# A two-layer attention kernel on one core: new orders for all engines' instruction lists

## What is computed

```python
xf = x.reshape(b, c, n)                       # n = 1024
q = einsum('rc,bcn->brn', Wq, xf) + bq        # 16 rows
k = einsum('rc,bcn->brn', Wk, xf) + bk        # 16 rows
v = einsum('oc,bcn->bon', Wv, xf) + bv        # 128 rows
energy = einsum('bri,brj->bij', q, k)         # 1024 x 1024
attn = softmax(energy, axis=2)
out = gamma * einsum('bcj,bij->bci', v, attn) + x
```

## Time and profile before

| | |
|---|---|
| median of 3 runs | 193.89 us (193.38 to 194.21) |
| the profiled execution | 193.06 us, span 191.3 us |
| TensorE busy | 179.1 us (94% of the span) |
| VectorE busy | 145.7 us (76%) |
| ScalarE busy | 155.5 us (81%) |
| GpSimd busy | 156.9 us (82%) |
| granted TensorE clock | 1.00 |

### The profile page before, as it was taken

The page is one execution under the profiler, slowest core; times in us unless marked ns, Lnnn a source line. Parts: engine busy times, 40 slices in busy tenths (PEclk is TensorE's granted clock), DMA queues, the critical chain, the costliest instruction groups (busy, mean ns, idle before and its releaser), DMA issues.

```text
span 191.3 us, 3482 instructions
## 1 busy us (share of the span) xinstructions
PE 179.1 (94%) x1282; PEld 123.1 (64%) x1282; DVE 145.7 (76%) x137; ACT 155.5 (81%) x223; POOL 156.9 (82%) x120
## 2 busy tenths in 40 slices
...
GB/s 155 345 104 0 215 9 42 69 3 3 2 113 0 5 111 3 0 3 3 110 3 0 3 55 58 2 3 107 61 55 7 55 0 58 3 0 55 55 55 55
DMA packets 3890, 9.51 MB, mean 50 GB/s; under 512 B 548, under 2 KB 932, under 8 KB 3876
## 3 DMA queue, kind: packets, MB, share of 16 engines
...
...
## 4 chain that ended last, share of the span: by engine, by line
PE 34%; POOL 31%; ACT 15%; issue 10%; DMA 4%; DVE 4%; SPq 1%; POOLq 0%; DVEq 0%; ACTq 0%
POOL attn_lo L364 14%; PE out_psum L720 10%; POOL attn_hi L359 9%; ACT ring L472 8%; PE out_psum L722 7%; ACT attn L484 4%; DMA qk_swapped<-qk 4%; PE ring L671 3%; PE ring L697 3%; PE out_psum L756 3%; PE ring L642 2%; DVE neg_max L563 2%; PE ring L624 2%; PE ring L657 2%; ACT attn_hi L490 2%
## 5 line engine op out<-in xcount | busy, mean ns | idle before, releaser
L364 POOL TENSOR_TENSOR attn_lo<-attn,attn_hi 128x1024 fp32r<-128x1024 f32 x37 | 90.4, 2455 | 1.8 <-ACT attn_hi L490 1.3
L563 DVE TENSOR_REDUCE neg_max<-ring 128x1 f32<-128x1024 f32 x64 | 75.6, 1219 | 15.7 <-PE ring L673 15.3
L472 ACT ACTIVATE ring<-ring,neg_max 128x1024 f32<-128x1024 f32 x64 | 69.6, 1087 | 9.9 <-DVE neg_max L563 9.3
L484 ACT ACTIVATE attn<-ring 128x1024 f32<-128x1024 f32 x64 | 63.3, 1024 | 9.8 <-DVE attn_lo L558 5.6
L359 POOL TENSOR_SCALAR attn_hi<-attn 128x1024 fp32r<-128x1024 f32 x35 | 39.2, 1134 | 5.5 <-ACT attn L484 5.4
L699 PE MATMUL ring<-qk_swapped,qk 64*128 64x512 f32 x64 | 29.0, 478 | 0.0
L697 PE MATMUL ring<-qk,qk_swapped 64*128 64x512 f32 x64 | 28.5, 468 | 0.3
L671 PE MATMUL ring<-qk_swapped,qk 64*128 64x512 f32 x56 | 25.1, 452 | 3.4 <-ACT attn L484 1.7
L673 PE MATMUL ring<-qk,qk_swapped 64*128 64x512 f32 x56 | 25.7, 461 | 0.0
L558 DVE TENSOR_TENSOR attn_lo<-attn,attn_hi 128x1024 fp32r<-128x1024 f32 x11 | 19.4, 1778 | 5.5 <-POOL attn_hi L359 4.7
L723 PE MATMUL out_psum<-attn_hi,v_hi 64*128 64x512 f32 x72 | 23.0, 399 | 0.0
...
## 6 DMA issues: line engine op xcount, KB each, us to landing
...
qk<-shift_rows SPq DMA_DIRECT2D x7, 8.0 KB
```

The lines of the kernel that those rows point to most:

```text
L364: nc.gpsimd.tensor_tensor(attn_lo[:, k - 1], attn[:, k], attn_hi[:, k - 1].bitcast(fp32), ALU.subtract).then_inc(cut_made["lo", "gpsimd"], 1)
L472: nc.scalar.activation(e[:], e[:], ACT.Exp, bias=neg_max[s][:, i:i + 1], accum_out=row_sum[s][:, i:i + 1]).then_inc(sum_made, 1)
L484: nc.scalar.activation(attn[:, k], ring_tile("ET", s, k)[:].rearrange("p (a n) -> p a n", a=2), ACT.Exp).then_inc(attn_made, 1)
L563: nc.vector.tensor_reduce(neg_max[s][:, i:i + 1], ring_tile("E", s, i)[:], axis=AX.X, op=ALU.max, negate=True).then_inc(max_made, 1)
```

## The change

Only the five lists are changed, and no function. The same stages, tiles and numbers are computed. Counted by kind and engine:

| | hi | lo | v_hi | v_lo |
|---|---|---|---|---|
| ScalarE | 13 to 4 | | 5 to 4 | |
| GpSimd | 35 to 44 | 37 to 32 | 3 to 4 | 5 to 4 |
| VectorE | | 11 to 16 | | 3 to 4 |

The warm entries ask for 16 pairs of matmuls where they asked for 18. All other kinds stay on their engine in the same number, in another order. In stage 0 the first two energies are E.0.2 and E.0.1, where they were E.0.6 and E.0.0, and QX.1 stands before them. Cut to the two ends of each list:

```diff
 PE_ORDER = """
-raw.0.0.0 raw.0.1.1 E.0.6.2 QX.1.0.0 E.0.0.1 QK.1.0.0 E.0.7.2 warm.0.2 E.0.4.0 E.0.2.1 E.0.1.2 warm.0.2 E.0.3.0
-E.0.5.1 VX.0.0.2 warm.0.2 E.1.4.0 V.0.0.2 shift.0.0.1 warm.0.2 E.1.7.1 warm.0.2 QX.2.0.0 E.1.6.2 QK.2.0.0 warm.0.2
-ET.0.2.1 warm.0.4 ET.0.3.2 warm.0.2 E.1.5.1 ET.0.1.0 E.1.0.2 PH.0.2 E.1.2.0 PH.0.3 shift.0.1.1 E.1.3.2 ET.0.0.1
...
-PV.7.1 PV.7.3 PH.7.5 PH.7.4 PV.7.6 PV.7.5 PV.7.4 PV.7.7
+raw.0.0.0 raw.0.1.1 QX.1.0.2 E.0.2.0 QK.1.0.2 E.0.1.1 warm.0.2 E.0.6.2 E.0.7.0 E.0.0.1 warm.0.2 E.0.3.2 E.0.5.0
+E.0.4.1 warm.0.1 VX.0.0.2 E.1.4.0 V.0.0.2 shift.0.0.1 warm.0.2 E.1.5.1 warm.0.2 QX.2.0.0 E.1.0.2 QK.2.0.0 warm.0.1
+ET.0.1.1 warm.0.4 ET.0.0.2 warm.0.2 shift.0.1.1 ET.0.3.0 E.1.3.1 VX.1.0.2 ET.0.2.0 V.1.0.2 PH.0.1 ET.0.7.0 E.1.7.1
...
+PV.5.4 E.7.2.0 E.7.1.1 PV.5.7 ET.6.6.2 PH.5.5 PV.5.6 PV.5.5 VX.7.0.0 ET.6.7.2 E.7.6.1 V.7.0.0 PH.6.6 PH.6.2 PH.6.4
+ET.6.5.2 shift.7.1.0 ET.6.1.1 PV.6.4 PV.6.7 PV.6.0 ET.7.5.0 ET.7.6.1 ET.7.4.2 PV.6.6 PH.6.5 PH.6.1 PV.6.5 ET.7.2.1
+ET.7.1.2 ET.7.7.0 PH.6.3 PV.6.1 PV.6.2 ET.7.0.2 ET.7.3.0 PV.6.3 PV.7.7 PH.7.6 PV.7.0 PH.7.3 PH.7.5 PH.7.4 PH.7.1
+PH.7.2 PV.7.1 PV.7.5 PV.7.3 PV.7.2 PV.7.4 PV.7.6
 """
 ACT_ORDER = """
-sum.0.6 evac.1.0 sum.0.0 sum.0.7 sum.0.4 sum.0.2 sum.0.1 sum.0.3 log.0.0 sum.0.5 sum.1.4 v_hi.0.0 log.0.1 sum.1.7
-sum.1.6 attn.0.2 attn.0.3 attn.0.1 sum.1.5 sum.1.0 sum.1.2 attn.0.0 sum.1.3 sum.1.1 sum.2.4 attn.0.6 log.1.1 sum.2.7
...
-attn.6.4 attn.6.1 attn.6.6 sum.7.5 log.7.1 hi.6.6 hi.6.4 attn.6.3 attn.6.7 attn.7.3 v_hi.7.0 attn.7.2 hi.7.2
-attn.7.0 attn.7.1 attn.7.6 attn.7.7 attn.7.5 attn.7.4 hi.7.5 hi.7.4
+evac.1.0 sum.0.2 sum.0.1 sum.0.6 sum.0.7 sum.0.0 sum.0.3 sum.0.5 log.0.0 sum.0.4 log.0.1 sum.1.4 sum.1.5 sum.1.0
+attn.0.1 attn.0.0 attn.0.3 attn.0.2 sum.1.3 attn.0.7 attn.0.4 sum.1.7 sum.1.1 sum.1.6 sum.1.2 sum.2.4 log.1.1
...
+sum.7.6 log.7.1 attn.6.1 attn.6.5 attn.7.6 attn.7.4 attn.7.5 attn.7.1 attn.7.7 attn.7.0 attn.7.3 attn.7.2 hi.7.3
 """
 DVE_ORDER = """
-max.0.6 max.0.0 max.0.7 max.0.4 max.0.2 max.0.1 max.0.3 max.0.5 max.1.4 rows.0.0 v32.0.0 max.1.7 max.1.6 mask.2.0
...
-max.7.7 v_lo.6.0 finish.5.1 max.7.5 v32.7.0 lo.6.5 rows.7.1 lo.6.6 lo.6.3 lo.6.4 finish.6.0 v_lo.7.0 lo.7.2
-finish.6.1 lo.7.6 lo.7.5 finish.7.0 finish.7.1
+max.0.2 max.0.1 max.0.6 max.0.7 max.0.0 max.0.3 max.0.5 max.0.4 max.1.4 rows.0.0 v32.0.0 max.1.5 max.1.0 mask.2.0
...
+finish.5.0 max.7.3 v32.6.0 max.7.2 max.7.1 v_lo.6.0 finish.5.1 max.7.6 v32.7.0 lo.6.6 rows.7.1 lo.6.2 lo.6.5
+v_lo.7.0 lo.6.1 finish.6.1 finish.6.0 lo.7.5 lo.7.1 lo.7.3 lo.7.4 finish.7.0 finish.7.1
 """
 POOL_ORDER = """
-mask.1.0 stack.1.0 parts.0.0 parts.0.1 v_lo.0.0 hi.0.2 hi.0.3 hi.0.1 lo.0.2 lo.0.3 lo.0.1 parts.1.1 hi.0.6 lo.0.6
...
-hi.5.5 hi.5.6 lo.5.5 lo.5.6 hi.6.2 hi.6.1 hi.6.5 parts.7.1 lo.6.2 hi.6.3 lo.6.1 hi.7.3 lo.7.3 hi.7.1 lo.7.1 hi.7.6
-lo.7.4
+mask.1.0 stack.1.0 parts.0.0 parts.0.1 v_hi.0.0 v_lo.0.0 hi.0.1 hi.0.3 hi.0.2 lo.0.3 lo.0.2 hi.0.4 lo.0.4 parts.1.1
...
+hi.5.6 lo.5.6 hi.6.3 lo.5.5 hi.6.2 hi.6.4 lo.6.3 hi.6.6 lo.6.4 parts.7.1 v_hi.7.0 hi.6.1 hi.6.5 hi.7.6 hi.7.5 lo.7.6
+hi.7.4 hi.7.2 hi.7.1 lo.7.2
 """
 SP_ORDER = """
-swap.1.0 swap.0.0 place.0.0 swap.2.0 place.0.1 place.1.1 swap.3.0 place.2.1 swap.4.0 place.3.1 swap.5.0 place.4.1
-swap.6.0 place.5.1 store.4.0 swap.7.0 store.4.1 place.6.1 store.5.0 store.5.1 place.7.1 store.6.0 store.6.1
+swap.0.0 swap.1.0 place.0.0 place.0.1 swap.2.0 place.1.1 swap.3.0 place.2.1 swap.4.0 place.3.1 swap.5.0 place.4.1
+swap.6.0 place.5.1 store.4.0 swap.7.0 place.6.1 store.4.1 store.5.0 store.5.1 place.7.1 store.6.1 store.6.0
 store.7.0 store.7.1
 """
```

More of the change, by code:

```diff
@@ L57 @@
[L57 to L71, removed]
```

54 lines of the change are left out of this document (33 added, 21 removed).

## The result

The changed kernel took **195.49 us** (median of 5 runs, 195.16 to 195.84) beside 193.38 for the kernel before on the same chip: a ratio of 1.0103, with a 95% interval from 1.008 to 1.0127. It is 1% slower where 1.4% faster was forecast, and outside the range. The profiled execution has a span of 193.4 us, 2.1 more than before.

What follows compares the result with a forecast made beforehand. Start, middle and tail were taken as bound by different things, the middle by nearly full TensorE, GpSimd and ScalarE. Start -2.0, middle +0.8 and tail -1.6 gave -2.8, a median of 191.1 us; 8-in-10 range 189.0 to 194.9.

Steps and rivals of the forecast that it cites:

- Start: Up to GpSimd's first hi: QX of stage 1 first brings evac, log.0.1 and the first attn forward; -2.0 us.
- three sums in 4.8 us: Start, ScalarE: attn is reached three sums of stage 1 after log.0.1, from about 22.9 to about 27.7 us.
- I cost the three separately and add them: Whole kernel: start, middle and tail are bound by different things, so their differences add, to -2.8 us.
- -1.1 of work: Middle, GpSimd's list: more hi, but fewer lo, v_hi and v_lo, make its work 1.1 us less.
- +3.2 for five turns: Middle: five more VectorE subtractions with both inputs in SBUF cost GpSimd 0.65 to 0.7 us each, +3.2.
- -1.3 of relief: Middle: ScalarE, 4.4 us lighter, gives back half of GpSimd's 2.7 us of waiting for attn, -1.3.
- Tail: From log.7.1 to the last matmuls: hi and lo ahead of stage 7's shift shorten waits; -1.6 us.
- no waits but these: Tail: a step-by-step walk gave -2.4 us; two thirds were taken, since it held only the waits it named.
- Rival (c): Middle: turns cost their whole 1.0 us and GpSimd gets nothing back; middle +4.0, total 194.3 us; chance 0.21.
- My signs for it: Middle: VectorE's L558 mean above 2.0, or GpSimd's hi above 1.3, would mean rival (c) or (d).
- Rival (d): Middle: VectorE becomes the bound through its added lo and v_lo, middle +6.9, total 197.2 us; chance 0.16.
- (b): Whole kernel: everything fits, GpSimd's 2.7 us of waiting goes, the tail gives 2.4; -5.0, 188.9 us; chance 0.13.

Runs made afterwards that it cites:

- e1: Changed kernel with 19 of VectorE's 20 subtractions turned into same-length maxima over one SBUF input, so no turns against GpSimd: 190.77 us, ratio 0.9868.
- e2: Kernel before with all 14 of VectorE's subtractions turned into same-length maxima over one SBUF input: 191.01 us, ratio 0.9888.
- f4: Kernel before with six of GpSimd's lo cut to 64 of 1024 columns, some 13 us of its work: 190.89 us, ratio 0.9853.
- e7: Kernel before with ScalarE's 12 hi of stages 1 to 7 cut to 64 of 1024 columns: 193.27 us, ratio 1.0002.
- e6: Changed kernel with only VectorE's subtractions of stages 6 and 7 (8 of 20 turns) turned into maxima over one input: 194.04 us, ratio 1.0037.
- g1: Changed kernel with ten hi given back from GpSimd to ScalarE at places where ScalarE waits: 196.61 us, ratio 1.0173.
- e9: Kernel before with five lo and a v_lo moved from GpSimd's list to VectorE's, nothing else: 196.19 us, ratio 1.0144.
- e3: New lists up to stage 0's second shift, the kernel before's lists for all that is left: 200.07 us, ratio 1.0347 to the kernel before.
- e4: Kernel before's lists up to stage 0's second shift, new lists for all that is left: 208.64 us, ratio 1.0801 to the kernel before.

## Why the prediction was wrong

**Start.** The mechanism was right: log.0.1 came at 23.22 for 22.9 forecast. The size was off by half: -0.9, not -2.0. The first energy, which was to come 0.2 earlier, came 0.25 later, at 10.27, behind a first projection that began 0.3 later, and the first attn at 29.04 for 27.9. Part of this is chance, since the first projection begins between 4.9 and 5.7 us in these traces and the first energy of the new lists between 9.5 and 10.9. What follows repeats itself: from the first energy to the first attn are 19.9 us in each of the eleven traces with the old start and 18.8 in each of the nine with the new one. So the new start is worth 1.1. The term that was too large is the way from log.0.1 to attn: I had three sums in 4.8 us, and it took 5.8, since ScalarE waited 2.1 us in all for the maxima of these sums (0.51, 1.24 and 0.35).

**Adding the three parts.** "I cost the three separately and add them" counts what the start gains in full at the end. The runs don't bear that out: e1's first hi is 1.3 before e2's, and their log.7.1 come together, at 159.72 and 159.77.

**Middle, GpSimd's list.** The forecast had three terms, -1.1 of work, +3.2 for five turns and -1.3 of relief. Taking the turns away took 3.8 us off the changed kernel's middle (132.7 against e1's 128.9) and 1.7 off that of before (129.4 and 127.7), so the new turns cost 2.1, for the 3.2 of the forecast: right in kind, and too large. What is left without turns is +1.2 where the two other terms said -2.4. This is the larger miss. The work saved had no value of its own: in all GpSimd is 3.1 us less busy in e1 than in e2 (145.4 and 148.5), and e1 isn't faster; f4 gives a fifth of what it takes away.

**Middle, ScalarE's relief.** This is the step that failed most plainly: "should give half of that back, -1.3". e7 shows that in the kernel before it is worth 0.0 (interval -0.5 to +0.6 us). I had read GpSimd's 2.7 us of waiting for attn as ScalarE being late with its work. ScalarE itself waits for TensorE's ring, 16.6 us in the changed kernel, and GpSimd's waiting for it grew, to 7.4 in the middle, though ScalarE had less to do.

**Tail.** -1.6 was forecast and -0.3 measured. The 5.56 us wait for lo.6.3 is gone, as I said, and ScalarE's first attn of stage 7 comes 8.2 us after log.7.1 (171.07) for 9.5 before. But e1 and e2 have equal tails, 29.3 us, so turns cost 1.5 in the old tail and 1.3 in the new one: the one lost turn that I took out was replaced. At 162.62 VectorE's lo.6.6 begins and takes 2.23, and behind it the first step of parts.7.1, 0.20 long otherwise, takes 1.18. TensorE waits 0.65 for these parts, and ScalarE 3.24 for ET.6.1, which stands behind them in TensorE's list. Without the turns of stages 6 and 7 (e6) TensorE is 1.4 us earlier by 168, and it keeps 1.2 of that. My walk through the new tail had "no waits but these", and that is the step that failed.

**The rivals.** Rival (c), the lock at its full price, had the mechanism and the side, 194.3 with 0.21, and lies 1.2 from the measured median where the forecast lies 4.4 (as differences to the kernel before, +0.4 and -2.8 for +2.1). That it lies so near is partly luck: its middle of +4.0 was 0.7 too dear, and it kept the -2.0 and -1.6 of the forecast. My signs for it missed it: VectorE's lo has a mean of 1.50 in the middle stretch, below the 2.0, and GpSimd's hi 1.10, below the 1.3. The lock stands as the Trainium skill's page SBUF — State Buffer has it, section "Who interferes with whom": in g1's rows VectorE's lo waits for the end of the lo that GpSimd began before it, and in the changed kernel's rows GpSimd's second lo waits for VectorE's. Rival (d), VectorE as the bound, isn't what happened, but e9 shows its mechanism in one place, a shift's rows queued behind a subtraction. My argument for (b), that lists are laid for such costs, was no argument from the profile.

What stays open: where between TensorE's order and the latency of a stage the lead of the start is lost and the 1.2 us of the new middle without turns arise (e3 and e4 were to show it and could not).
